# One addition of the third edge stage done by GpSimd between its gathers, and VectorE's scaling of a message moved ahead of its adding up

## The reference, cut to what matters

```python
hn = _mlp(node_z, ...)                    # 32 values a node
he = _mlp(edge_z, ...)                    # 32 values an edge
msg = concatenate([hn[src], he])          # 64 values an edge
emb_edge = _mlp(msg, red_ln_w, red_ln_b, red_W, red_b)
msg_sum = segment_sum(emb_edge, dst)      # add up at each target
# _mlp(x, w, b, W, c): (x - mean) * rsqrt(var + eps) * w + b, then @ W.T + c, then leaky_relu(., 0.01)
```

## Time and profile before

| | us |
|---|---|
| timed, median of 3 runs | 4991.14 (4990.61 to 4994.25) |
| span of the profiled execution (its own time; no other is recorded for it) | 5820.0 |
| third edge stage, about | 1120 of the span |
| busy in that stage: DVE, PE, POOL, ACT | 818, 783, 612, 457 |

### The profile page before, as it was taken

The page is one execution under the profiler, slowest core; times in us unless marked ns, Lnnn a source line. Parts: engine busy times, 40 slices in busy tenths (PEclk is TensorE's granted clock), DMA queues, the critical chain, the costliest instruction groups (busy, mean ns, idle before and its releaser), DMA issues. The chain is left out here.

```text
span 5820.0 us, 104938 instructions
## 1 busy us (share of the span) xinstructions
PE 4388.1 (75%) x29528; PEld 2834.6 (49%) x29528; DVE 4126.9 (71%) x7954; ACT 2011.5 (35%) x6556; POOL 3270.2 (56%) x2950
## 2 busy tenths in 40 slices
PE   2999899989677777756777777376777667549998
PEld 1444444444344444445555555244444434349998
DVE  4767676766777676767777777466666666789998
ACT  2656566666000000134434444000000000057775
POOL 4666666663566666455555554455555555325554
PEclk6999999999788888778888888688888888779998
DMA  4333333331212111121111111233333333211111
GB/s 114 91 90 94 87 87 93 94 87 48 52 43 44 40 43 44 23 47 45 45 42 47 44 45 35 63 101 103 100 103 101 105 106 102 78 43 47 49 49 33
DMA packets 493105, 394.00 MB, mean 68 GB/s; under 512 B 346007, under 2 KB 379168, under 8 KB 492904
## 3 DMA queue, kind: packets, MB, share of 16 engines
q1 hardware_dynamic: 395496, 303.53, 18.3%
q0 software_dynamic: 90560, 83.37, 8.0%
q10 hardware_dynamic: 6976, 6.23, 0.3%
HBM read 355.34 MB, written 37.42 MB: 67 GB/s over the span
## 5 line engine op out<-in xcount | busy, mean ns | idle before, releaser
L1093 POOL DMA_INDIRECT edge_src_rows<-table_wh,edge_gather_idx x806 | 867.8, 1077 | 503.0 <-issue 229.7
L950 POOL DMA_INDIRECT edge3a_src_rows<-table_h,edge3a_gather_idx x808 | 763.1, 944 | 632.7 <-issue 259.0
L2165 PE MATMUL edge3a_z_ps<-Wz,edge3a_both_ends_t 128*128 128x396 f32 x1616 | 736.3, 600 | 405.0 <-DVE edge3a_terms L2258 322.0
L1123 PE MATMUL edge_sums_ps<-edge_onehot_src,edge_halves 128*128 128x512 bf16 x4840 | 890.0, 331 | 43.2 <-issue 32.4
L950 POOL DMA_INDIRECT table_cat<-table_hn,table_gather_idx x592 | 624.9, 1056 | 479.6 <-PE edge_sums_ps L1795 181.2
L1508 POOL DMA_INDIRECT edge_src_rows<-table_h,edge_gather_idx x608 | 609.1, 1002 | 424.4 <-issue 175.4
L2258 DVE SCALAR_TENSOR_TENSOR edge3a_terms<-edge3a_z_ps,att_z 128x792 f32<-128x792 f32 x404 | 386.1, 977 | 486.6 <-DMA edge_edge_attr<-in_ea 307.5
L2165 PEld LDWEIGHTS edge3a_z_ps<-Wz,edge3a_both_ends_t 128*128 128x128 f32 x1616 | 346.6, 226 | 733.7 <-DVE edge3a_terms L2258 368.3
L1123 PEld LDWEIGHTS edge_sums_ps<-edge_onehot_src,edge_halves 128*128 128x128 f16 x4840 | 385.6, 97 | 477.4 <-issue 69.5
L2577 PE MATMUL edge3b_sums_ps<-edge3b_onehot,edge3b_weighted 128*128 128x128 f32 x4848 | 572.9, 279 | 6.3 <-DVE layers_accT L2615 4.4
L2577 PEld LDWEIGHTS edge3b_sums_ps<-edge3b_onehot,edge3b_weighted 128*128 128x128 f32 x4848 | 553.6, 193 | 12.0 <-DVE layers_accT L2615 4.6
(11 more groups left out here) (370 smaller groups left out, 7950.6 us busy)
## 6 DMA issues: line engine op xcount, KB each, us to landing
edge_dst_row<-in_dst_row SPq DMA_DIRECT2D x102, 512.0 KB
edge3a_dst_row<-in_dst_row SPq DMA_DIRECT2D x102, 512.0 KB
edge_window<-table_wh_parts SPq DMA_DIRECT2D x816, 48.8 KB
edge3a_window<-table_h SPq DMA_DIRECT2D x816, 32.0 KB
edge_edge_attr<-in_ea SPq DMA_DIRECT2D x101, 256.0 KB
kept_rows<-edge3a_src_rows SPq DMA_DIRECT2D x101, 256.0 KB
edge3b_src_rows<-kept_rows SPq DMA_DIRECT2D x101, 256.0 KB
edge_edge_attr<-in_ea SPq DMA_DIRECT2D x101, 128.0 KB
```

The lines of the kernel that those rows point to most:

```text
L950: nc.gpsimd.indirect_dma_start(self.slot(b, j), None, self.table[:, :], bass.IndirectOffsetOnAxis(ap=self.idx[b][:, j:j + 1], axis=0)).the ...
L1093: nc.gpsimd.indirect_dma_start(g[q][:, j, :], None, k.t_wh[:, :], bass.IndirectOffsetOnAxis(ap=idx[q][:, j:j + 1], axis=0)).then_inc(gathe ...
L1123: mm = pe.matmul(acc[:, i, 0:w], halves[q][:, j, a, :, :].rearrange("p h d -> p (h d)"), hot[:, o:o + w], start=first and a == 0, stop=False)
L2165: mm = pe.matmul(zp[q % 2][:, i, 0:H * ZH], hcT[h][:, j * P:(j + 1) * P], k.Wz[:, :], start=True, stop=True)
```

## The change

`message` is cut in two on DVE: `scale` (reciprocal and L1981) now stands ahead of the eight additions, `finish` (the leaky ReLU) where the message stood. The addition of the constant row between them is done by GpSimd (`shift`), from `u` and the constant row in SBUF. It issues it between the fourth and the fifth gather of the batch that is four later, ahead of the wait that stands there, and for a batch 3, which has no gathers, behind the eighth gather of the batch before. The last four messages are shifted when all gathers are out. The copy of the constant row to PSUM goes.

```diff
-        row, ec, rc = fixed[:, 0:P].unsqueeze(1), fixed[:, P:P + HALF], fixed[:, 2 * P:2 * P + D]
+        row, ec = fixed[:, 0:P].unsqueeze(1), fixed[:, P:P + HALF]
...
             def _(pool):
+                def shift(n):
+                    pool.wait_ge(u_sc, n)
+                    nc.gpsimd.tensor_tensor(u2[:, :, :], u[:, :, :], rows_over(k.rc[:, :], B),
+                                            ALU.add).then_inc(u_b, 1)
+
                 def midway(pool, t, h, q, m, j):
+                    if j and live_shift(t, h):
+                        shift(2 * t + h - 3)
                     if h == 1:
...
-                ga.loop(nc, pool, begun=True, midway=midway)
+
+                def live_shift(t, h):
+                    return not isinstance(t, int) or 2 * t + h >= 4
+
+                def body(t, q, m):
+                    if isinstance(t, int) and t == 0:
+                        return
+                    for h in (0, 1):
+                        if not used_batch(t, h):
+                            continue
+                        ga.gather(nc, pool, t, h, q, m, midway=midway)
+                        if 2 * q + h == TAKEN and live_shift(t, h):
+                            shift(2 * t + h - 3)
+                by_parity(pool, body)
+                for n in range(USED - 3, USED + 1):
+                    shift(n)
...
-                dve.tensor_copy(rc, k.rc[:, :]).then_inc(row_ready, 1)
...
-                def message(n, h):
+                def scale(n):
                     dve.wait_ge(std2_ready, n)
                     dve.reciprocal(st[:, 5, :], st[:, 4, :]).then_inc(inv2, 1)
                     dve.wait_ge(inv2, n)
                     dve.tensor_tensor(u[:, :, :], rp[:, :, 0:D], over(st[:, 5, :], D),
                                       ALU.mult).then_inc(u_sc, 1)
-                    dve.wait_ge(u_sc, n)
-                    dve.tensor_tensor(u2[:, :, :], u[:, :, :], rows_over(rc, B),
-                                      ALU.add).then_inc(u_b, 1)
+
+                def finish(n, h):
                     dve.wait_ge(u_b, n)
                     dve.scalar_tensor_tensor(msg[h][:, :, 0:D], u2[:, :, :], 0.01, u2[:, :, :],
                                              ALU.mult, ALU.max).then_inc(msg_ready, 1)
...
                         if b == TAKEN:
                             take(m, 0)
+                        if not (first and h == 0):
+                            scale(n - 1)
                         if not first:
                             add(n - 2, h, t - 1, m + (b == TAKEN), due(t, m, b))
...
                         if not (first and h == 0):
-                            message(n - 1, 1 - h)
+                            finish(n - 1, 1 - h)
```

More of the change, by code:

```diff
@@ L1912, in _ @@
                 dve.tensor_copy(ec, k.ec[:, :]).then_inc(row_ready, 1)
-                dve.tensor_copy(rc, k.rc[:, :]).then_inc(row_ready, 1)
                 dve.memset(msg[0][:, :, D], 1.0)
                 dve.memset(msg[1][:, :, D], 1.0).then_inc(ones_ready, 1)
-                dve.wait_ge(row_ready, 3)
+                dve.wait_ge(row_ready, 2)
                 step = Chain(dve, prep)
@@ L2033, in body @@
                         if not (first and h == 0):
-                            message(n - 1, 1 - h)
+                            finish(n - 1, 1 - h)
                 by_parity(dve, body)
                 onehot(dve, k, oh[0][:, :, :], PAIRS - 1, 0, row).then_inc(oh_ready, 1)
+                scale(USED)
                 add(USED - 1, 1, PAIRS - 2)
-                message(USED, 0)
+                finish(USED, 0)
                 add(USED, 0, PAIRS - 1)
```

## The result

The changed kernel takes 5030.85 us (5027.11 to 5034.54, 4 runs) against 4990.88 us (4988.85 to 4994.25, 4 runs) for the one before: 1.0078 times as long, 95% interval 1.0065 to 1.0091. It is slower, by 40 us where 25 were forecast.

A forecast was written before the change was run, and what follows sets the result against it. Engines passing batches along bound the third edge stage; GpSimd's chain becomes longest: 11.75 + 0.92 + 25.5 + 0.74 = 38.9 us a group against 37.9, over 25.25 groups 25 us: 4991 + 25 = 5016 us, eight in ten 4925 to 5075.

The forecast's parts named there:

- The first profile's gaps: Third edge stage: PE's 8.2 us for 13 products and VectorE's 7.60 us hole, taken as costs of the recorded execution.
- The group after: Third edge stage: four batches in the changed kernel take 38.9 us timed, against 37.9 before.
- The chain of sixteen gathers and three additions: GpSimd, from its restart in the fourth batch to the group's second message: 16 x 1.36 + 3 x 1.25 = 25.5 us.
- the ring: Third edge stage: engines pass one batch along, each idle 20 to 45%; the measured loop of one group took 39.35 us.
- The addition's price: GpSimd's 128x512 constant addition: 0.92 us, plus 0.30 us ahead of it, counted as 1.25 us each.
- The holds: GpSimd's additions blocking VectorE's SBUF-only instructions in the third edge stage: 0 to 46 us, none added to the forecast.
- the relief: VectorE loses the constant's addition: 2.16 us a group, 1.24 net of the moved scaling, 31 us; stage busy time down about 70.
- The move: Scaling ahead of the eight additions: PE's tile free 3.6 us earlier, no gain counted; minus 0.92 us in the fourth batch.
- The third rival: PE is the real bound and gets its tile earlier: 3.2 us a group, 80 us faster, 4911 us; chance 0.10.
- The first: Rival: GpSimd keeps up, gathers under 1.22 us, VectorE's savings count: 31 us faster, 4960 us; chance 0.26.
- The second: Rival: GpSimd's added work and VectorE's savings cancel within 0.2%, or hide behind PE: 4991 us; chance 0.19.
- The fourth: Rival: GpSimd's addition costs 2.4 us, sign over 1.5 us: 5.5 us a group, 139 us slower, 5130 us; chance 0.09.

The follow-up runs named there:

- the second profile: The kernel before, unchanged, profiled once more: 4985.8 us with the profile, span 4984.0 us; the first recorded execution had spanned 5820.0 us.
- the three runs with fewer gathers: Changed kernel, two of 24 gathers a group left out: around the first message's GpSimd addition, one each side 5001.36 us, both ahead 5033.7, both behind 4974.78.
- the small addition: Changed kernel, but GpSimd adds the constant to one tile of eight only and the leaky ReLU reads the scaled message; all waits stay: 4967.91 us, 0.9955 of before.
- Two additions in four: Changed kernel, but GpSimd adds the constant for only two messages of a group, VectorE for the two that had waited: 4988.81 us, 0.999 of before.

## Why the prediction was right, and where its steps were off

**The first profile's gaps.** Taking them for a cost of the recorded execution was the choice on which the sign hung, and the second profile bears it out. Scaling the group by the whole kernel's ratio gave 37.9 us, where it is 37.43: that stage was lengthened more than the rest. These 0.5 us are 12 of the 15 us between forecast and result.

**The group after.** Forecast 38.9, measured 38.98. Its pieces fared less well. From the fourth batch's first L1963 to GpSimd's restart 12.67 us were forecast and 12.54 measured (2707.22 to 2719.76). The chain of sixteen gathers and three additions was put at 25.5 us and takes 26.2, but with its wait of 1.43 us; its own work is 24.7. Gathers are nearer to their 1.25 than to 1.36 us. So the step "there lie sixteen gathers and three additions" failed as a bound: the three runs with fewer gathers show eight of them on the ring, the rest of it running over VectorE, PE and ScalarE. The two ways were within 1.4 us of each other, which is why the number held. That is in part luck: a path that does not bind, with gathers counted too long (1.36 us for 1.29), came out as long as the ring that does, whose additions were priced too low and whose hold was put at nothing.

**The addition's price.** 0.92 us from L2494's 1.8 ns an element was too low: 1.274 us, and the gather behind it takes 1.40 to 1.47 in place of 0.95. With 0.16 us of issue an addition takes 1.43 from start to start, and the gather behind it has its successor 1.77 us later (2725.97 to 2727.74) in place of 1.25, 0.5 more; the gather ahead of it is followed 0.3 us sooner (2723.57 to 2724.53 us, 0.96 in place of 1.25). Put between two gathers it thus costs 1.7 us, against the 1.25 counted (where 0.92 + 0.30 is 1.22). Timing GpSimd from start to start was right: the eight gathers between 2734.13 and 2744.66 have a distance of 1.32 us on average, where their spans are about 1.05. The Trainium skill (Perfetto Trace Analysis, GPSIMD Engine Instruction), by which a span there is unreliable, agrees.

**The holds.** Counted as none, "as DVE is then not the longest chain". The size was bounded well (0 to 46 us; 325 one-hots at 621 against 477 ns are 47), the place was not: two one-hots a group are stretched (1.68 and 1.18 us above), and the first stands between L1984 at 2719.76 and L2002 at 2731.94, where VectorE hardly idles, ahead of the addition that waits. This term was put at nothing because VectorE was not on the longest chain; two thirds of the ring, 26 of 39.3 us, lie on VectorE, PE and ScalarE, and the small addition shows the one stretched one-hot there costing 1.2 us a group, 30 us. Two additions in four shows such holds eating up the relief. The Trainium skill (Advanced Engine Details and Errata, VectorE Performance Modes, Mode Summary) says that VectorE's second SBUF port is shared with GpSimd, and that GpSimd's instructions and VectorE's two-port ones block each other. The trace agrees for the one-hots, and VectorE's instructions with an operand in PSUM keep their length beside GpSimd's additions: the additions of sums 0.28 us, the scaling 0.69, the one-hot matrix L982 1.21.

**The move.** Net of the moved 0.92 us no gain was counted for PE's earlier tile. Alone it brings 18 us, and 40 without the fourth batch; the 0.92 us between the two L1957 were rightly called a loss (0.8 to 0.9 a group). The third rival was right that PE's wait is worth something, and wrong on its size (80 us): the wait went on to the sums, and which part of the gain comes from PE's granted clock is open.

**The relief.** 2.16 us a group were to go from VectorE. Its stage busy time fell by 27 us, not 70: 69 removed (73 from start to start), 47 given back by the holds, and the 5 left over lie in other lines, 1.6 of them in the leaky ReLU. The relief was worth next to nothing even with a small addition on GpSimd.

**The rivals.** The first (GpSimd keeps up) needed gathers under 1.22 us. The second falls by the interval, which excludes no change. The fourth's mark was an addition over 1.5 us; 1.27 is short of it. GpSimd idles 82 us behind its waits for PE and VectorE from 2220 to 3205, 3.3 us a group, under the 5 us that would have spoken against the chain. Two figures of the prediction don't come out of its own rows: the 431 us of GpSimd's waits are of 1040 and not of 980 us, and an addition dearer by half a microsecond, three times a group, puts the upper end of the forecast's own range at 5054, not 5045; neither carries the forecast. The span of 5790 us for a profile as lengthened as the first could not be tested: the profile after was not lengthened.

**What stays open.** Why before stands at 37.4 us and the move alone at 36.6 to 36.8 a group is known only in parts: not GpSimd, and the stretch between the two L1957 is a loss of the move and no part of its gain. PE's granted clock, 0.87 and 0.92, is the rival that no run tried. Nor was GpSimd's addition tried together with the move in three batches.

## What to carry to other kernels

Before work is given to an engine that waits often, lay out its instructions from start to start against the time of one round, from the point at which its input is made to the point at which its output is wanted; idle time elsewhere does not help. Look at what the two engines do to each other while both run, since that cost falls on instructions that nobody moved, and ask of each such instruction whether it lies on the ring. And run the parts of a change apart: here the move of two instructions, in three batches of four, was the gain (0.9917), and the work given away was the loss.

## What the runs showed of the hardware

- A GpSimd f32 addition of 128x512 takes 1.274 us and of 128x64 0.330: 2.1 ns an element and 0.2 us ahead. The 128x1920 of the earlier trace rows is 1.8 ns an element.
- The indirect gather that follows such an addition without a wait takes 1.40 to 1.47 us, not 0.95; behind a wait it takes 0.96 (2719.76). It is not the only cause of a long gather: in the second profile of before, without additions, one took 1.97 us (2611.65).
- VectorE's 128x1024 f16 one-hot, 0.476 us alone, takes up to 1.87 us in the changed kernel when it meets a GpSimd addition, mostly 1.18 and 1.68: the one at 2724.42 began 0.11 us before the addition and was held for 1.20 of its 1.28 us.
- It can be the other way round: with the 128x64 addition the one-hots keep their 0.477 us, and the addition beside them takes 1.21 us instead of 0.33, once a group (2434.48 in that run).
- PE's 16 products of L1856 take 1.16 us at a granted clock of 1.00 (2.4 GHz) and 2.08 at 0.50 (1.2 GHz), where PE had idled 3.93 us just before.
- A profiled execution can be 17% longer than the timed runs of the same kernel and its other profile (5820 us, 4991 and 4984), with idle time put down to issue between matrix products that follow without a gap elsewhere.
